# A softmax-maximum hand-over on one Trainium2 core: its two subtractions move from GpSimd to VectorE, and its steps are placed one unit apart

## What is computed

```python
def attend(x, Wq, Wk, Wv, Wo, mask_or_weight):      # 16 heads of width 16
    Q, K, V = heads(x @ Wq.T + bq), heads(x @ Wk.T + bk), heads(x @ Wv.T + bv)
    scores = einsum("bhqd,bhkd->bhqk", Q, K) / 4
    return softmax(scores, masked or weighted) @ V, then @ Wo.T + bo

a = attend(x, ..., "prior": listed keys, or a dense bias, by a flag per batch)
x = x + attend(a, ..., "causal")
x = x + ffn(mixer(x))        # gated mixer with three scans; mixture of 8 experts plus a shared FFN
```

## Time and profile before

| | |
|---|---|
| median of 3 runs | 1694.05 us (1690.55 to 1695.26) |
| the profiled execution | 1694.05 us, its span 1692.3 us |
| busy share of the span | PE 92%, DVE 53%, ACT 43%, POOL 42% |
| first and last of the 32 POOL steps L1130 | 111.1 and 999.8 us |
| attention ends, FFN begins | about 1050 us |

### The profile page before, as it was taken

The page is one execution under the profiler, slowest core; times in us unless marked ns, Lnnn a source line. Parts: engine busy times, 40 slices in busy tenths (PEclk is TensorE's granted clock), DMA queues, the critical chain, the costliest instruction groups (busy, mean ns, idle before and its releaser), DMA issues. The chain is left out here.

```text
span 1692.3 us, 20420 instructions
## 1 busy us (share of the span) xinstructions
PE 1564.3 (92%) x7328; PEld 763.0 (45%) x7376; DVE 892.1 (53%) x2047; ACT 726.7 (43%) x990; POOL 704.1 (42%) x515
## 2 busy tenths in 40 slices
PE   5789999778999999898989888999999999999998
PEld 3423333222333333343343323545666577777755
DVE  7678878789767865646755553334322111111141
ACT  4754665445466565466645557133221111111110
POOL 5437999867789999233211111310000300000070
PEclk9569999998999999999998988999999999999999
DMA  3460123131313220334432013300040004334061
GB/s 102 141 156 25 34 70 70 58 91 45 92 54 72 56 58 22 77 91 110 125 89 57 25 36 112 112 5 0 1 149 1 26 1 149 122 114 157 16 123 27
DMA packets 75905, 121.43 MB, mean 72 GB/s; under 512 B 14920, under 2 KB 53265, under 8 KB 72731
## 3 DMA queue, kind: packets, MB, share of 16 engines
q1 hardware_dynamic: 72155, 113.62, 23.6%
q0 software_dynamic: 3072, 6.03, 2.1%
q10 hardware_dynamic: 576, 0.47, 0.1%
HBM read 85.08 MB, written 36.96 MB: 72 GB/s over the span
## 5 line engine op out<-in xcount | busy, mean ns | idle before, releaser
L1140 POOL TENSOR_TENSOR sb_prob<-sb_prob,sb_weight 128x1024 f32<-128x1024 f32 x192 | 450.8, 2378 | 64.8 <-ACT sb_prob L1347 64.4
L1347 ACT ACTIVATE sb_prob<-wide 128x1024 f32<-128x1024 f32 (+3 forms) x384 | 347.7, 917 | 242.8 <-PE wide L1957 139.2
L1952 PE MATMUL wide<-sb_stack_q,sb_stack_k 99*128 99x512 bf16 (+3 forms) x896 | 284.5, 366 | 27.5 <-DVE sb_prob L1676 14.0
L1634 DVE CUSTOM_DVE_ANT_0 sb_junk<-bank,sb_bias 128x512 bf16<-128x512 f32 x348 | 232.0, 687 | 56.0 <-PE bank L1925 53.6
L1391 ACT ACTIVATE sb_sil<-wide 128x320 f32<-128x320 f32 (+1 forms) x128 | 66.2, 518 | 437.7 <-PE wide L2031 437.7
L1925 PE MATMUL bank<-sb_stack_k,sb_stack_q 96*128 96x512 bf16 (+3 forms) x604 | 219.4, 381 | 25.9 <-DVE sb_rowmax L1634 13.9
L2031 PE MATMUL wide<-sb_weight,sb_ffn 128*128 128x512 f32 x512 | 234.1, 601 | 0.0
L1972 PE MATMUL wide<-sb_prob,sb_v_aug 128*17 128x512 f32 (+3 forms) x1792 | 223.4, 566 | 8.4 <-ACT sb_o_raw L1360 7.0
L1768 DVE TENSOR_TENSOR sb_act_s<-sb_sil,wide 128x512 f32<-128x512 f32 x64 | 44.0, 687 | 254.4 <-ACT sb_sil L1391 254.4
L1628 DVE TENSOR_REDUCE sb_rowmax<-bank 128x1 f32<-128x512 f32 (+3 forms) x256 | 134.5, 550 | 67.9 <-PE bank L1928 51.9
L1178 POOL DMA_INDIRECT sb_weight<-slots_out,sb_slot_r x32 | 31.4, 980 | 284.9 <-issue 281.3
(11 more groups left out here) (264 smaller groups left out, 1850.5 us busy)
## 6 DMA issues: line engine op xcount, KB each, us to landing
sb_stack_k<-parts SPq DMA_DIRECT2D x32, 256.0 KB, 6.9
o_raw<-sb_o_raw SPq DMA_DIRECT2D x32, 256.0 KB, 2.3
sb_big<-rg SPq DMA_DIRECT2D x8, 1024.0 KB, 4.9
sb_big<-ru SPq DMA_DIRECT2D x8, 1024.0 KB, 7.6
sb_big<-rd SPq DMA_DIRECT2D x8, 1024.0 KB, 10.8
sb_stack_q<-parts SPq DMA_DIRECT2D x16, 384.0 KB, 4.9
parts<-sb_o_norm SPq DMA_DIRECT2D x40, 128.0 KB
sb_stack_q<-parts SPq DMA_DIRECT2D x16, 256.0 KB, 5.5
```

The lines of the kernel that those rows point to most:

```text
L1140: e.tensor_tensor(p, p, weight_of(*u[1:]), ALU.mult).then_inc(weigh_p.handle, 1)
L1347: e.activation(p[:, :, first:HALF], sc[:, :, first:HALF], ACT.Exp).then_inc(SC.empty_sem(u), 1)
L1634: e.tensor_tensor_reduce(out=junk[:, i % 2, 0:hi - lo], in0=BK.tile(u)[:, 0:hi - lo], in1=bias[:, qt, lo:hi], scale=1.0, scalar=-3e38, op0 ...
L1952: i = e.matmul(sc[:, j * HALF + first:(j + 1) * HALF], stack_k[0:ROWS_M, n % 3, g, kt * P:(kt + 1) * P], stack_q[0:ROWS_M, n % 3, g, half ...
```

## The change

Steps 2 and 4 go from POOL to DVE. There the subtraction is one scalar_tensor_tensor: rem = (top * -1) - part 0, and rem2 = (rem * 1) - part 1. The sign now turns in step 2, so ACT's steps 3 and 5 copy with scale 1 where they had -1. Both sources lie in SBUF, one float32, one bfloat16, 32 elements a partition. `FIN_AT` goes: step k stands at k units after `LEAD`, `turn` at 7 as before. Steps 2 and 4 thus stand a unit later; the others stay.

```diff
-FIN_AT = (0, 1, 1, 3, 3, 5, 6, 7)
...
-        out += [(LEAD + FIN_AT[k] / units_of(n), u) for k, u in enumerate(steps) if u]
+        out += [(LEAD + k / units_of(n), u) for k, u in enumerate(steps) if u]
...
-        top_d = signal("dve_top", [u for u in of("fin") if u[2] == 0])
-        rest_p = signal("pool_rest", [u for u in of("fin") if u[2] in (2, 4)])
+        top_d = signal("dve_top", [u for u in of("fin") if u[2] % 2 == 0])
...
-                elif u[0] == "fin" and u[2] in (2, 4):
-                    _, n, k = u
-                    part = mpart[:, n % 2, :, :, k // 2 - 1].rearrange("p n h -> p h n")
-                    w.wait_ge(top_a.after(("fin", n, k - 1)))
-                    if k == 4:
-                        w.wait_ge(rest_p.after(("fin", n, 2)))
-                    e.tensor_tensor(mneg[:, k // 2], mneg[:, k // 2 - 1], part, ALU.add).then_inc(rest_p.handle, 1)
...
-                    w.wait_ge((rest_p if k > 1 else top_d).after(("fin", n, k - 1)))
-                    e.activation(part, (top, rem, rem2)[k // 2], ACT.Copy, scale=-1.0).then_inc(top_a.handle, 1)
+                    w.wait_ge(top_d.after(("fin", n, k - 1)))
+                    e.activation(part, (top, rem, rem2)[k // 2], ACT.Copy,
+                                 scale=-1.0 if k == 1 else 1.0).then_inc(top_a.handle, 1)
...
+                    elif k == 2:
+                        w.wait_ge(top_a.after(("fin", n, 1)))
+                        e.scalar_tensor_tensor(out=rem, in0=top, scalar=-1.0, in1=part[0], op0=ALU.mult,
+                                               op1=ALU.subtract).then_inc(st, 1)
                     else:
+                        w.wait_ge(top_a.after(("fin", n, 3)))
+                        e.scalar_tensor_tensor(out=rem2, in0=rem, scalar=1.0, in1=part[1], op0=ALU.mult,
+                                               op1=ALU.subtract).then_inc(st, 1)
```

More of the change, by code:

```diff
@@ L1636, in _ @@
                         op0=ALU.add, op1=ALU.max, accum_out=acc).then_inc(BK.empty_sem(u), 1)
-                elif kind == "fin" and u[2] == 0:
+                elif kind == "fin" and u[2] % 2 == 0:
                     _, n, k = u
[L1639 to L1647, removed]
-                    else:
-                        e.tensor_reduce(top, rowmax[:, n % 2], AX.X, ALU.max).then_inc(st, 1)
+                    top, rem, rem2 = (mneg[:, i] for i in range(3))
+                    part = [mpart[:, n % 2, :, :, i].rearrange("p n h -> p h n") for i in range(2)]
+                    st = top_d.handle
+                    if k == 0:
+                        for mark in [BK.emptied(v) for v in MAXES[n][-2:]]:
+                            w.wait_ge(mark)
+                        if n:
+                            w.wait_ge(top_a.after(("fin", n - 1, FIN_STEPS - 1)))
+                        if JOBS[n][0]:
+                            e.tensor_reduce(top[:, :, 0:NT // 2], rowmax[:, n % 2, :, 0:NT // 2, 0:1], AX.X, ALU.max)
+                            e.tensor_reduce(top[:, :, NT // 2:NT], rowmax[:, n % 2, :, NT // 2:NT, :], AX.X,
+                                            ALU.max).then_inc(st, 1)
+                        else:
+                            e.tensor_reduce(top, rowmax[:, n % 2], AX.X, ALU.max).then_inc(st, 1)
+                    elif k == 2:
+                        w.wait_ge(top_a.after(("fin", n, 1)))
+                        e.scalar_tensor_tensor(out=rem, in0=top, scalar=-1.0, in1=part[0], op0=ALU.mult,
+                                               op1=ALU.subtract).then_inc(st, 1)
+                    else:
+                        w.wait_ge(top_a.after(("fin", n, 3)))
+                        e.scalar_tensor_tensor(out=rem2, in0=rem, scalar=1.0, in1=part[1], op0=ALU.mult,
+                                               op1=ALU.subtract).then_inc(st, 1)
```

## The result

The changed kernel is slower: 1711.59 us (median of 4 runs, 1704.13 to 1715.85) against 1692.3 us for the kernel before (also 4 runs), a ratio of 1.0107 with a 95% interval from 1.0075 to 1.0139. That lies above the predicted range (1688 to 1703), on the slow side. The profiled execution took 1709.51 us, with a span of 1707.8 us.

The account below looks back on a forecast made before the run. TensorE was at 92%, but POOL set the pace where it had no gap, DVE next fullest in jobs 3 and 4. Terms -0.2 + 0 + 2.3 + 0.6 - 1.5 + 0 = +1.2 on 1694.05 gave 1695.2 us, range 1688 to 1703.

Parts of the forecast that it names:

- the price of a two-source step: DVE's new steps beside POOL: each waits until POOL's running instruction ends, the longest near 2.4 us.
- The mean wait: Hand-overs 1 to 8: 1.04 us for each of 16 DVE steps, in all 16.7 us of DVE standing still.
- Where POOL has no gap ... I take the two together at 0.: Gapless POOL stretches: DVE's waits and POOL's relief from its short steps taken together at 0, bounds -2.1 and +2 us.
- ACT's wait at job 8: Hand-over to job 8: ACT no longer stands 3.91 us for POOL's queue; -1.5 us, bounds 0 and -4.7.
- Places: All hand-overs: steps 2 and 4 standing one unit later change nothing, 0 us, bounds -1 and +1.
- Jobs 3 and 4: Hand-overs in 318 to 483 us: DVE's waits, together 5.8 us, reach TensorE in part; +2.3 us, bounds 0 and +5.8.
- The causal jobs: 669 to 1008 us: 16 DVE steps of up to 0.18 us, a fifth of 2.9 us felt; +0.6, bounds 0 and +2.9.
- The first hand-over: Job 0, where all engines wait for the chain: two steps each shorter by about 0.1; -0.2 us, bounds -0.4 and +0.2.
- The FFN: After 1050 us nothing of the change exists, so its 642 us stay.
- The slow rival: Hand-overs 1 to 8: DVE's waits reach TensorE everywhere, share 0.69 of 16.7 us; +10.4 us, 1704.4; chance 0.21.

Follow-up runs that it names:

- the paired source: Changed kernel, but DVE's steps 2 and 4 add maximum and ACT's part, side by side in one float32 SBUF tile; 0.9983 of the kernel before.
- the dummy source: Changed kernel, but DVE's steps 2 and 4 are a maximum over a tile of zeros, subtraction left out; 0.9984 of the kernel before, 1689.2 us.

## Why the prediction was wrong, by its steps

**The step that failed** is the price of a two-source step: "I read this as a wait until POOL's running instruction ends", from the 2.26 us at 390.03 and the longest of 2.82. Those rows come from jobs 3 and 4, where POOL has gaps (it is busy for 125.0 of 165 us) and these instructions meet it at most in the 7th instruction since a gap of over 0.3 us. The mean wait built on it (1.04 us each) was then applied to jobs 1, 5 and 7, where the earlier trace rows showed POOL at nine tenths and more. There the step was asked for during the 14th, 14th and 19th instruction of a gapless run, 26.7, 26.7 and 43.8 us after its start, and waited for the run's end: 6.73, 6.75 and 7.32 us. In the earlier trace rows no case of that sort exists, and I had taken the longest case seen as the longest possible. The Trainium skill's rule (SBUF — State Buffer, section "SBUF: two separate sides") is that whichever starts first holds the shared pair for its whole instruction. That each excludes the other agrees with the trace (2.38 us at 613.95); it says nothing on who follows when both wait, and that was the loss.

**"Where POOL has no gap ... I take the two together at 0."** It came to +13.9 us (7.34 + 6.59, the hand-overs to jobs 2 and 6). The thought behind it was that a late DVE only costs TensorE time that it would have waited for POOL. For waits of one boundary no run contradicts it (the 26 other steps: 0.15 points, not told apart from nothing); it can't hold for a wait that by its nature lasts until POOL's backlog is gone, since that backlog was the cover.

**ACT's wait at job 8, -1.5 us.** The old stall did vanish, but a 7.32 us step took its place: +1.0 us instead. Its worth was undersized too. In the kernel with the paired source the transposes for job 8 gain 5.97 us on those for job 7, with the dummy source 5.91 us, both more than my bound of 4.7. Of this the whole kernel kept little: 0.9983 is some 3 us, and not told apart from nothing. Other places gave part back (+1.96 us on the way to job 3, for one).

**Places, 0 (-1 to +1).** The term was undersized, with the wrong sign. For the steps on DVE, which are those of the change, the new places were a gain: 1.0107 against 1.0194 with two sources, 0.9983 against 1.0017 with one. For POOL's steps they cost 0.5%, which is 0.0051 x 1692 = 8.6 us (4.9 to 12.3); the change doesn't pay this, since POOL has no steps. I had followed DVE's and ACT's queues, and not what a unit holds in POOL's.

**What held.** Jobs 3 and 4: the steps waited 2.09, 0.20, 0.21 and 1.85 us, and the transposes for job 5 lost 0.9 us on those for job 3 (forecast +2.3, bounds 0 to 5.8), less than single executions differ by. The causal jobs: -0.8 us from job 8's transposes to the FFN (forecast +0.6, bounds from 0), too small to call. The first hand-over: -0.9 (forecast -0.2), but the runs give -1.3 to +1.2 there for hardly different kernels. The FFN did not change (638.5 us against 639.7). The slow rival had the right engine and the right victim, but neither the place nor the price: not a share of sixteen mean waits, but three long ones.

**Open.** Alone, the limit lay between the 14th and the 16th of half-length instructions, and between the 15th and the 16th of full ones. In the kernel the two steps at the 14th were already passed over, in the changed one and in both others that had them there. POOL's run there mixes four instructions of 1.15 us with ten of 2.36, and its waits are on several semaphores; which of it lowers the limit wasn't tried.

How long a gap must be for the count to begin anew was not varied either. Alone 0.31 us was enough. In job 6 of the changed kernel 0.07 or 0.05 us seems to have been: step 2 was let in on the 7th instruction since the one and the 4th since the other, but on the 25th since the last longer gap; the kernel with the old places has the same picture (2.41 us). In the kernel in which POOL waits, the run in job 6 had no such gap: step 2 came on the 28th instruction and stood for the 6.43 us shown above. So the count explains the stall that moved there.

## What to carry to other kernels

A wait read from rows is a bound only for the load that those rows saw: before a short instruction moves beside an engine with a backlog, look for rows in which that engine had one just as long. On this chip keep DVE instructions with two SBUF sources out of long gapless runs of POOL, or give them one source in SBUF (the other operand in PSUM, or both numbers in one tile and a reduction), which was let in at once in every run here. And a step moved "one unit later" moves by whatever its own engine's queue holds in that unit.

## What the runs showed of the hardware

- A two-source DVE instruction that finds POOL running is let in at the next instruction boundary if POOL's gapless run is young (67 of 68 stand-alone cases up to the 15th instruction, and one boundary later in the case that asked 0.07 us before an end), and stands until the run ends if it is asked for during the 16th or later (all 23, up to 34.97 us). Which of the two depended on the number of instructions since POOL's last gap, not on the time since (16.4 us let in and 18.8 us passed over with half-length instructions, 33.7 us let in with full ones), on whether the rest was released ahead, or on ACT's copies and DMAs beside it.
- In the kernel this began at the 14th instruction already (6.73 to 7.13 us in place of 0.2); why is open.
- An idle time of 0.31 us in POOL's run resets the count.
- A DVE instruction with one source in PSUM (0.19 us) or a single SBUF source (0.22 us) is not held up at all, also in the 19th instruction of a run. A small two-source step that is let in does not delay POOL visibly; one of 128x512, which took 2.51 us, delayed it by 0.45 us.
- A bfloat16 written into the upper half of a zeroed float32 word can be read as float32 by the next instruction: two operands become one source, for 0.02 us more on DVE (0.226 against 0.210 us).
